# A decoder layer of attention, retention and top-3 experts on one core: five edits to waits, orders and a row pitch

## The reference

```python
x = x + attn(ln(x))           # 16 heads of 64, causal, rms norm first, gated by sigmoid(x @ Wg), all in float32
x = x + retention(ln(x), ctx) # 16 heads of 8, q from x, k and v from ctx, decay masks, no softmax
x = x + experts(ln(x))        # 12 experts 128 -> 512 -> 128 with erf gelu; each token's top 3, weighted by softmax
```

## Time and profile before

| what | us |
|---|---|
| median of 3 runs | 562.97 |
| lowest and highest of them | 560.76, 564.37 |
| the profiled execution, its own time | 557.62 |
| its span, first to last instruction | 555.8 |
| busy: PE, DVE, ACT, POOL | 482.0, 393.8, 340.4, 281.2 |
| loop period of batches 2 to 6 | 44.8 |

### The profile page before, as it was taken

How to read it: one execution, slowest core, us unless ns; L and a number is a source line. 1 busy time by engine, 2 the same in 40 slices (tenths; PEclk the granted TensorE clock), 3 DMA queues, 4 the chain that set the end, 5 groups by cost and what they waited for, 6 DMA issues and landing times.

```text
span 555.8 us, 12676 instructions
## 1 busy us (share of the span) xinstructions
PE 482.0 (87%) x3683; PEld 397.1 (71%) x3683; DVE 393.8 (71%) x1324; ACT 340.4 (61%) x1012; POOL 281.2 (51%) x432
## 2 busy tenths in 40 slices
PE   2799999989998998998998999687975899999990
PEld 1567777776785885786677678456665899988880
DVE  4665668878877987887887888776983555445546
ACT  3568766766865865875776686253462666666650
POOL 3400033584375286278258447722748575565554
PEclk9989999999999999999999999778978799999996
DMA  8200000010010000000000001056554687776676
GB/s 269 83 2 1 1 2 2 1 38 0 0 33 5 0 24 14 0 14 24 0 9 29 0 0 39 1 157 174 162 111 138 184 219 214 204 190 197 186 203 153
DMA packets 58196, 42.87 MB, mean 77 GB/s; under 512 B 5059, under 2 KB 51447, under 8 KB 58160
## 3 DMA queue, kind: packets, MB, share of 16 engines
q1 hardware_dynamic: 53904, 35.42, 23.6%
q0 software_dynamic: 3824, 6.49, 3.6%
q10 hardware_dynamic: 432, 0.53, 0.4%
HBM read 31.70 MB, written 12.16 MB: 79 GB/s over the span
## 4 chain that ended last, share of the span: by engine, by line
PE 46%; DVE 19%; issue 10%; ACT 10%; another core or an unknown queue 5%; POOL 4%; SPq 3%; DMA 1%; DVEq 0%; ACTq 0%; POOLq 0%
PE zb L740 8%; PE sc L779 6%; PE ob L808 5%; PE xb L857 4%; PE xb L882 3%; PE tb_a L740 2%; PE ob L994 2%; ACT pT L613 2%; ACT p_sb L606 2%; PE tb_b L740 2%; PE tb_a L792 2%; PE tb_b L792 2%; PE sc L773 2%; PE zb L994 2%
## 5 line engine op out<-in xcount | busy, mean ns | idle before, releaser
L486 POOL TENSOR_TENSOR spare_p<-tri 128x1 f32<-128x1 f32 x94 | 26.6, 283 | 121.2 <-DVE xn L1187 67.0
L597 ACT ACTIVATE qk<-zb 128x512 f32<-128x512 f32 x64 | 38.2, 597 | 74.9 <-PE zb L740 74.9
L563 POOL DMA_INDIRECT results_by_token<-y_sb,row_i x70 | 69.9, 998 | 22.0 <-issue 19.9
L604 ACT ACTIVATE p_sb<-sc,nmx 128x128 f32<-128x128 f32 x128 | 47.0, 367 | 29.5 <-DVE nmx L1106 29.1
L779 PE MATMUL sc<-qk 64*128 64x256 f32 (+1 forms) x512 | 61.9, 362 | 0.2 <-ACT qk L597 0.2
L606 ACT ACTIVATE p_sb<-sc,nmx 128x256 f32<-128x256 f32 x128 | 61.0, 476 | 0.0
L779 PEld LDWEIGHTS sc<-qk 64*128 64x128 f32 x512 | 46.0, 194 | 16.3 <-issue 10.4
L508 POOL DMA_INDIRECT tokens_by_expert<-packed,slot_i x48 | 52.9, 1103 | 8.5 <-issue 7.5
L808 PE MATMUL ob<-pT,v_sb 128*64 128x256 f32 (+1 forms) x512 | 56.4, 342 | 0.9 <-DVE oT L1124 0.9
L1124 DVE TENSOR_TENSOR oT<-ob,pT 128x256 f32<-128x256 f32 x64 | 26.9, 420 | 36.8 <-PE ob L808 25.4
L808 PEld LDWEIGHTS ob<-pT,v_sb 128*64 128x64 f32 x512 | 31.4, 137 | 19.8 <-issue 8.8
(11 more groups left out here) (272 smaller groups left out, 1446.1 us busy)
## 6 DMA issues: line engine op xcount, KB each, us to landing
wup_sb<-in_L_ffn_Wup SPq DMA_DIRECT2D x35, 256.0 KB
wdn_sb<-in_L_ffn_Wdown SPq DMA_DIRECT2D x35, 256.0 KB
xg<-tokens_by_expert SPq DMA_DIRECT2D x35, 130.0 KB
tokens_by_expert<-padding SPq DMA_DIRECT2D x12, 260.0 KB
results_by_token<-y_sb,row_i POOLq DMA_INDIRECT x70
wkv_sb<-in_L_attn_Wkv SPq DMA_DIRECT2D x2, 512.0 KB, 6.4
ctx_b<-in_ctx SPq DMA_DIRECT2D x8, 128.0 KB
out<-x_all SPq DMA_DIRECT2D x4, 256.0 KB, 2.3
```

The lines of the kernel that those rows point to most:

```text
L563: pool.indirect_dma_start(out=ys, out_offset=bass.IndirectOffsetOnAxis(ap=row_i[:, u, a:a + 1], axis=0), in_=y_sb[:, u, a, :], in_offset=None,
L597: act.activation(qk[:, :, :].rearrange("p h j -> p (h j)"), zb[:, :], ACT.Copy).then_inc(a_qk, 1)
L604: act.activation(p_sb[:, w, h, 0:P], sc[:, k, S:S + P], ACT.Exp, bias=nmx[:, w, 0, n:n + 1], accum_out=total[:, w, 0, h:h + 1])
```

## The change

- `ROW` becomes D + 16: rows of 576 bytes. The 14 floats behind the weight are set to zero once.
- PE's `x_T(nxt)` at s = 3 stands in front of `weigh`.
- DVE's root `deviation(link, brs)` moves from s = 4 to s = 5, and `ratio(cur, 5)` from the head of s = 6 to s = 5, in front of the root.
- `load(n)` waits for a new semaphore `f_row` (row numbers and weights copied out of `xg`), issues up weights and rows (`ld_e`), then waits for `f_dn` and issues down weights (new `ld_d`), for which `down` waits. DVE copies the weights to a small tile `weight`.
- POOL's scatters of result tiles 0 and 1 move between the last dispatches of batch 6; of that batch's sends only the order around the retention of batch 7 changes.

```diff
-ROW = D + 2
+ROW = D + 16
@@ load(n), SP
-                    sp.wait_ge(f_y, n - DEPTH + 1)
+                    sp.wait_ge(f_row, n - DEPTH + 1)
...
                 sp.dma_start(wup_sb[:, u, :], ...).then_inc(ld_e[u], 16)
-                sp.dma_start(wdn_sb[:, u, :, :], ...).then_inc(ld_e[u], 16)
...
                 sp.dma_start(xg[:, u, :, :], ...).then_inc(ld_e[u], 16)
+                if n >= DEPTH:
+                    sp.wait_ge(f_dn, n - DEPTH + 1)
+                sp.dma_start(wdn_sb[:, u, :, :], ...).then_inc(ld_d[u], 16)
@@ POOL
+            pool.memset(packed[:, :, :, D + 2:ROW], 0.0)
...
-            dispatch(B - 2, pace_last)
-            pack(B - 1)
-            dispatch(B - 1)
-            for n in range(TILES):
+            begin(B - 2)
+            for n in range(3):
+                send(B - 2, n)
+            queries(B - 1)
+            send(B - 2, 3)
+            retained(B - 1, 0)
+            scatter(0)
+            send(B - 2, 4)
+            keep(B - 1)
+            send(B - 2, 5)
+            scatter(1)
+            pack(B - 1)
+            dispatch(B - 1)
+            for n in range(2, TILES):
+                scatter(n)
@@ up_high (ACT), turn_tokens (PE)
-                act.wait_ge(ld_e[u], (n // DEPTH + 1) * 48)
+                act.wait_ge(ld_e[u], (n // DEPTH + 1) * 32)
-                pe.wait_ge(ld_e[u], (n // DEPTH + 1) * 48)
+                pe.wait_ge(ld_e[u], (n // DEPTH + 1) * 32)
@@ step (PE)
-                if (w := lagged(cur, prev, s, 2)) and (cur is not None or s < 2):
-                    weigh(*w)
                 if s == 3 and nxt is not None:
                     pe.wait_ge(a_qk, at(cur, PAIRS, s + 2))
                     x_T(nxt)
+                if (w := lagged(cur, prev, s, 2)) and (cur is not None or s < 2):
+                    weigh(*w)
@@ down (PE)
+                pe.wait_ge(ld_d[u], (n // DEPTH + 1) * 16)
@@ step (DVE)
-                if (w := lagged(cur, prev, s, 1)) and (s != 2 if cur is not None else s < 1):
+                if (w := lagged(cur, prev, s, 1)) and (s not in (2, 6) if cur is not None else s < 1):
                     ratio(*w, link)
...
                 if prev is not None:
                     if s in (4, 5):
                         read_state(prev, s - 4, 1)
-                    if s == 4:
+                if cur is not None and s == 5:
+                    ratio(cur, 5, link)
+                if prev is not None:
+                    if s == 5:
                         deviation(link, brs)
@@ tokens, results (DVE)
                 dve.tensor_copy(row_i[:, u, :], xg[:, u, :, D].bitcast(I32))
+                dve.tensor_copy(weight[:, u, :], xg[:, u, :, D + 1]).then_inc(f_row, 1)
...
-                    ins = dve.tensor_scalar(y_sb[:, u, a, :], y_sb[:, u, a, :], xg[:, u, a, D + 1:D + 2], None, ALU.mult)
+                    ins = dve.tensor_scalar(y_sb[:, u, a, :], y_sb[:, u, a, :], weight[:, u, a:a + 1], None, ALU.mult)
```

More of the change, by code:

```diff
@@ L209, in decoder @@
         row_i = sb("row_i", [P, DEPTH, HALVES], I32)
+        weight = sb("weight", [P, DEPTH, HALVES])
         bdn_sb = sb("bdn_sb", [P, E, D])
@@ L261, in decoder @@
         ld_e = [sem(f"ld_e{u}") for u in range(DEPTH)]
+        ld_d = [sem(f"ld_d{u}") for u in range(DEPTH)]
         scattered = [sem(f"scattered{u}") for u in range(DEPTH)]
@@ L280, in decoder @@
         pe_CNT, v_hit, v_filled, v_slot, v_pad, v_first, v_plan, v_fin = (sem(n) for n in ("pe_CNT", "v_hit", "v_filled", "v_slot", "v_pad", "v_first", "v_plan", "v_fin"))
+        f_row = sem("f_row")
         f_T, f_hi, f_w, f_xg, f_up, f_gelu, f_dn, f_y, f_out = (
@@ L348, in load @@
                 sp.dma_start(wup_sb[:, u, :], f_wup[bass.ds(e, 1)].rearrange("a p n -> p (a n)")).then_inc(ld_e[u], 16)
-                sp.dma_start(wdn_sb[:, u, :, :], dn_v[bass.ds(e, 1)].rearrange("a p c d -> p (a c) d")).then_inc(ld_e[u], 16)
                 if n == 0:
@@ L356, in load @@
                 sp.dma_start(xg[:, u, :, :], xs[bass.ds(r, SLOTS), :].rearrange("(a p) w -> p a w", p=P)).then_inc(ld_e[u], 16)
+                if n >= DEPTH:
+                    sp.wait_ge(f_dn, n - DEPTH + 1)
+                sp.dma_start(wdn_sb[:, u, :, :], dn_v[bass.ds(e, 1)].rearrange("a p c d -> p (a c) d")).then_inc(ld_d[u], 16)
             sp.wait_ge(v_first, 1)
@@ L495, in pack, with send, begin @@
                 ins.then_inc(p_pack, 1)
-            def dispatch(b, pace=None):
+            def send(b, n):
+                t, k = divmod(n, TOPK)
+                pool.indirect_dma_start(
+                    out=xs, out_offset=bass.IndirectOffsetOnAxis(ap=slot_i[:, t, k:k + 1], axis=0),
+                    in_=packed[:, t, k, :], in_offset=None).then_inc(dispatched, 16)
+            def begin(b):
                 if b == B - 1:
@@ L502, in dispatch @@
                 carry(1)
+            def dispatch(b, pace=None):
+                begin(b)
                 for n in range(T * TOPK):
@@ L506, in dispatch @@
                         carry(3 + n)
[L507 to L510, removed]
+                    send(b, n)
             def keep(b):
@@ L544, in _, with scatter @@
             pack(B - 2)
[L546 to L551, removed]
-            dispatch(B - 2, pace_last)
-            pack(B - 1)
-            dispatch(B - 1)
-            for n in range(TILES):
+            def scatter(n):
                 u = n % DEPTH
```

## The result

The changed kernel takes 566.93 us in the median of 4 runs (565.42 to 568.11), the kernel before beside it 561.87 (559.97 to 564.37). The ratio is 1.0105, with an interval from 1.0058 to 1.0152. The profiled execution took 565.42 us, its span is 563.7. The forecast was 566.5 us. Its sum was made on the profiled execution of before, though, and there it said +3.5 us where 7.8 were measured (557.62 to 565.42); between the medians of four runs each it is +5.1. That the forecast meets the median to 0.5 us is therefore luck in part, and the terms have to be looked at one by one.

A forecast was written before the change was run, and what follows sets the result against it. PE was taken as the bound; -1.3 + 6.0 + 3.9 - 2.5 - 2.9 + 0.3 = +3.5 us on the profiled 557.6 gave 561.1. With 5.35 from profiled execution to median, 566.5 us, range 552 to 578.

The forecast's parts named there:

- The root: Loop batches 1 to 6: moved root closes 1.34 us, adds a 2.4 us PE stall in step 7; +6.0 us.
- The clock: Behind the step 7 stall: PE's clock falls in half of six batches, some 1.3 us each; +3.9 us.
- The next x: Loop batches 2 to 6: x_T ahead of weigh shortens PE's 1.48 us gap, -0.25 us each; -1.3 us.
- rival (1): PE's releases hang on POOL's runs, which end sooner; x and late stretch gain more, clock stays up: 555.6 us, chance 0.20.
- Batch 7: Root leaves step 4, early plan moves up, so the maxima of step 6 come sooner; -2.5 us.
- Loads and scatters: Expert stage: earlier rows of load 7 and an earlier late PE release to ACT; together -2.9 us.
- -0.4 for the rows of tile 7: Expert stage: load 7 issues its rows ahead of the down weights, shortening PE's wait; 0 to -0.74, taken as -0.4 us.
- +0.3 for the copies: One more tiny copy a tile, four on DVE's serial path up to the late plan; +0.3 us.
- The signs that were named: PE's gaps in steps 4, 5 gone; step 7 gap 2 to 2.5 us; loop period 45.5 to 47 us.
- (3): Stall lowers the clock in all six batches, x and late stretch give nothing, slack pace starts sooner: 576.9 us, chance 0.22.
- (2): Late part runs like the part before 468, its 5.7 us of idle time gone: 560.8 us, chance 0.12.
- (4): Root lies hidden in step 5 and all gaps go, batch 7 gives 5 us: 546.1 us, chance 0.08.

The follow-up runs named there:

- after_again: The changed kernel as it is, on one of the three other chips: 551.07 us against 539.20 for the kernel before, ratio 1.0222.
- rest_alone: The changed kernel with the root and x_T put back, leaving loads, scatters and row pitch: 540.64 us against 539.06 for the kernel before, ratio 1.0017.
- x_alone: The kernel before with only x_T moved in front of weigh: 538.79 us against 539.06, ratio 0.9987.
- scatters_alone: The kernel before with only the scatters of result tiles 0 and 1 moved between the last dispatches: 539.66 us against 539.58, ratio 1.0007.
- before_again: The kernel before, unchanged, run and traced on one of the three other chips: 537.91 us, one run.

## Why the prediction was right, and where its terms were not

**The root, +6.0 forecast, right in mechanism, low in size.** The maxima are late, the masks of step 7 wait, PE had come there earlier. The stall is 2.54 us (2.4), the cost without the clock 1.33 us a batch (1.0), so 8.0 us in six batches. The prediction's own rows came to 228.37 - 227.26 = 1.11, of which it took 1.0; of the rest, 0.09 is the longer stall, and 0.13 is that the closed gaps gave 2.54 - 1.33 = 1.21 us and not 1.34, the gaps themselves being 0.77 and 0.28 us there; so of the 0.30 us of restarting, which no row had shown, 0.16 was there. The 1.33 is read on other chips; the sum below supports it for this one.

**The clock, +3.9 forecast, some 7 measured; this is the term that was mis-sized.** A fall costs 1.45 us (1.3), the mean of what three kernels show. I took it in half of the batches; it was five of six in the changed kernel, and 13 of 18 over three kernels. "By the nearest row it falls each time" was nearer than the half that I took. It also fell a sixth time, in batch 7, which no term had (below).

**The next x, -1.3 forecast.** The gap in front of the first product fell from 1.48 to 0.17 us, and not for rival (1)'s reason, since POOL's run was still going when the turned x was read (219.05 against 219.68). The prediction's doubt, that the release comes with the end of that run, does not hold (that it hangs on the scatters in some other way is not excluded); its other reason for a small gain, that DVE has to be earlier too, does. 0.63 us came back in front of the state, since DVE's release (`oT`, at 220.46 after 2.41 us of "remote" idling) stayed late, 2.5 us behind the end of `weigh`, and 2.6 before. The late releases cost a batch of before 44.77 - 44.30 = 0.47 us, and a batch of the changed kernel whose clock fell 47.35 - 47.14 = 0.21 us, the second from after_again. So some 0.25 us a batch were given back there, the size that I took. That x did this is argued and not shown: the comparison crosses chips, and x alone did not run on the first one. On the others it gave nothing.

These three make 8.0 + 5 x 1.45 - 5 x 0.25 = 14.0 us, against a shift of 14.3 at the start of batch 7's states. The forecast had 8.6.

**Batch 7, -2.5 forecast, -2.0 measured** (14.3 to 12.4 at the maxima of step 6). POOL's products held the plan in place of the root, one of its operations 1.81 us, as the bound assumed:

```profile
372.14 1.81 DVE L1367 TENSOR_SCALAR first_plan<-rows,base 128x7 int32<-128x7 f32 x1
373.87 0.16 DVE L1138 RECIPROCAL rr<-total 128x4 f32<-128x4 f32 x1
```

Behind these maxima the stall stands in batch 7 too, and the clock falls with it:

```profile
383.62 0.28 PE L792 MATMUL sc<-mask,ident 128*128 128x256 bf16 x1 [2.46 <-ACT p_sb L625]
...
386.00:390.00 4.00, 4.00 (x22) 3.26 (x21) 3.20 (x19) 3.01 (x12) 0.00 (x0) 0.50 0.72 226
```

The shift rises to 12.9 at the output projection. There the kernel before has a fall of its own (0.57 from 382 to 386) and the changed one has not (1.00 from 394 to 398), and at tile 6 the shift is 11.5. So from the maxima to tile 6 another 0.8 us go, before any late load.

**Loads and scatters, -2.9 forecast, -4.9 measured**, all of it between tiles 7 and 8. The -0.4 for the rows of tile 7 was not there (5.90 us from tile 6 to tile 7, then 5.96). PE's idle time behind tile 7 and ACT's wait of 4.85 us shrank, and the clock is 1.00 there where before has 0.55 (426 to 436). As a whole the edits gave nothing on chips without late releases (rest_alone 1.0017), so the gain is likely tied to those; but on such a chip that distance also shrinks by 1.6 us in x_alone, which has none of these edits, and which edit does it on the first chip no run shows. "The two moved scatters cost 0" was wrong by 0.3 us on the landing of tile 7's rows (scatters_alone). The +0.3 for the copies is too small for these ratios to show.

**What no term had:** the clock's fall in batch 7, and +1.6 us behind the last tile. DVE's results of the last tile come at 551.79, 11.8 us behind the turning of that tile, where before has 543.28 and 9.6, with two idle stretches of DVE of 3.54 and 3.11 us, "remote" both; on the chip of before_again that end is the same in both kernels, 20.7 and 20.6 us. It was not pursued.

So +14.3 - 2.0 - 0.8 - 4.9 - 0.3 + 1.6 = +7.9, where the forecast had +3.5; the 0.8 is the rest of batch 7, and the 0.3 the tiles behind tile 8. The medians come out equal because I added the 5.35 us by which the median of before lay above its profiled execution, and that of the changed kernel lies only 1.5 above its own. A forecast made on one execution has that error in it, and here it made up for the clock and the root taken too low: the mechanism was right, the closeness of the number luck.

**The signs that were named.** The gaps in front of L797 and L882 are gone, the new gap of 2.54 us and the clock behind it are there, and so is DVE's copy without its wait. Three are not as named: the period is 47.35 us and not 45.5 to 47; ACT's `xN` is not released behind POOL's last scatter; and the stretch from 421 to 438 shrank by 5.5 us (shift +11.5 at 420.05, +6.0 at 437.98), which is more than the 5 that the prediction had named as a sign that it is wrong. So its account of the expert stage failed by its own measure, though that of the root, which carries the result, held.

**The rivals.** (3) was the nearest: the clock down in nearly all batches, though without its other parts. (1) came true in two of its signs (x's gap, the stretch behind tile 7), not in its reason for the first and not in the loop's sum. (2) did not: the slack pace stayed. (4) fell by the stall; but the idle time it hoped for exists in step 5, in another place.

## What to carry to other kernels

A chain of tiny dependent operations costs its whole length at whatever stands behind it, so before moving it look for the idle brackets of its own engine, and for the number of steps of PE's work between the last of them and the next result that another engine waits for: here twelve operations right ahead of the maxima lost 2%, and the same twelve one place earlier, under idle time, won 1.2%. A stall on PE is priced twice, by its length and by the clock behind it; where rows show both outcomes, take the clock's share in full for the upper end. Closing a gap is worth only the difference to the next one: 1.48 us of idle time was worth some 0.25.

## What the runs showed of the hardware

One chip ran the kernel before at 562 us, three others of its type at 539. What the traces show besides is releases that reach ACT and DVE late, in the loop of before 2.3 and 2.6 us behind the end of PE's instruction, and that are named "remote", each time in stretches with POOL's indirect transfers: 0.47 us a batch, and one tile in 3.86 us in place of 3.43 in the late part. Of the 19.6 us between the two profiled spans of before, 4.9 are there at tile 7, 9.5 at tile 8 and 18.2 at the last. On the three other chips no such release occurs in any of twelve kernels. What makes them late is open; no run took the transfers away on the chip that shows them, so that they hang on POOL is only what their times suggest, and the turned x of the changed kernel, released before the end of POOL's run, shows that they do not wait for that end.

The clock's fall behind a stall is not fixed by the stall: the same 2.54 us, ahead of the same instructions, had it in one batch and not in the next, at a price of 1.4 to 1.5 us each.
